# Nine weight buffers, six PSUM banks for the last expert job, per-tile turns, and a new order in a two-layer mixture-of-experts kernel

## The reference

```
x = x + L0_attn(L0_cond(x))        # attention with conditioning, then rotary attention (16 heads of 64)
x = x + L0_ffn(L0_cond2(x))        # quaternion filter, then 8 experts, top 2 of each token
x = x + L1_attn(L1_cond(x))        # 8 experts of three layers, top 2; then log-linear attention (8 heads of 128)
x = x + L1_ffn(L1_cond2(x))        # attention with conditioning, then a quantised FFN with a short convolution

# L0_ffn, a mixture: for each expert e
h = relu(x @ W1[e] + b1[e]);  y = h @ W2[e] + b2[e];  out += y * router_weight[:, e]
# L1_cond, a mixture: gate from rms-normalised x
h1 = relu(x @ W1[e]); h2 = relu(h1 @ W2[e]); out_e = h2 @ W3[e];  out = sum over the top 2
```

## Time and profile before

| | us |
|---|---|
| median of 3 runs (629.35, 630.21, 632.31) | 630.21 |
| the profiled execution, whole time | 623.68 |
| its span, first to last instruction | 621.9 |
| TensorE busy | 473.9 (76%) |
| VectorE busy | 303.5 (49%) |
| ScalarE busy | 246.2 (40%) |
| GpSimd busy | 171.4 (28%) |
| mean granted TensorE clock, share of full speed | 0.884 |

### The profile page before, as it was taken

One profiled execution on the slowest core, in us unless ns is written; L12 is line 12 of the kernel. 1 busy time (PEld: TensorE's weight loads), 2 busy tenths in 40 slices (PEclk: granted clock), 3 DMA queues, 4 the chain that ended last, 5 costly groups with the idle time before them and its releaser, 6 DMA issues.

```text
span 621.9 us, 11762 instructions
## 1 busy us (share of the span) xinstructions
PE 473.9 (76%) x4233; PEld 375.1 (60%) x4233; DVE 303.5 (49%) x771; ACT 246.2 (40%) x683; POOL 171.4 (28%) x210
## 2 busy tenths in 40 slices
PE   4897989768989946587776978669998734778875
PEld 4685877557869924466665866544665624566432
DVE  3779655643334427511122247774554003776653
ACT  3545644314575541123332463232554422343311
POOL 5054343172220233550004003455100022232200
PEclk9999989975999977769998998876999985897888
DMA  7977540010444530137786663101263710000000
GB/s 246 325 203 148 160 135 2 2 43 18 132 130 124 154 90 22 47 94 201 185 214 198 171 185 93 27 9 42 61 172 90 182 50 18 2 3 0 1 9 9
DMA packets 50631, 62.13 MB, mean 100 GB/s; under 512 B 6704, under 2 KB 39664, under 8 KB 50320
## 3 DMA queue, kind: packets, MB, share of 16 engines
q1 hardware_dynamic: 48048, 56.88, 33.1%
q0 software_dynamic: 2048, 4.20, 2.3%
q10 hardware_dynamic: 480, 0.32, 0.2%
HBM read 52.86 MB, written 16.94 MB: 112 GB/s over the span
## 4 chain that ended last, share of the span: by engine, by line
PE 55%; DVE 18%; issue 10%; ACT 10%; POOL 3%; another core or an unknown queue 2%; DMA 2%; ACTq 0%; POOLq 0%; DVEq 0%
PE PS L852 6%; PE PS L842 6%; PE PS L826 4%; PE PS L1407 4%; PE PS L1439 4%; PE PS L1834 3%; PE PS L1224 2%; PE PS L1238 2%; PE PS L1421 2%; DVE arena L1735 2%; PE PS L838 2%; PE PS L1213 2%; ACT rot_sm L1494 2%; ACT hid L920 2%
## 5 line engine op out<-in xcount | busy, mean ns | idle before, releaser
L766 POOL DMA_INDIRECT picked<-slots_y,place_u x32 | 31.1, 971 | 109.4 <-DMA slots_y<-slot_y 100.9
L852 PE MATMUL PS<-expert_w,hid 128*128 128x128 f32 x360 | 54.0, 287 | 7.6 <-ACT hid L920 2.7
L852 PEld LDWEIGHTS PS<-expert_w,hid 128*128 128x128 f32 x360 | 46.4, 196 | 14.4 <-issue 10.0
L1072 DVE TENSOR_SCALAR hid<-PS,expert_w 128x128 f32<-128x128 f32 x60 | 18.3, 347 | 75.3 <-PE PS L842 42.2
L842 PE MATMUL PS<-hid,expert_w 128*128 128x128 f32 x240 | 35.7, 296 | 12.5 <-ACT hid L920 9.9
L920 ACT ACTIVATE hid<-PS,expert_w 128x128 f32<-128x128 f32 x120 | 37.4, 366 | 16.7 <-PE PS L826 10.6
L842 PEld LDWEIGHTS PS<-hid,expert_w 128*128 128x128 f32 x240 | 31.3, 204 | 17.0 <-issue 15.8
L826 PE MATMUL PS<-slot_xT,expert_w 128*128 128x128 f32 x240 | 40.0, 293 | 1.9 <-ACT slot_xT L910 1.9
L1439 PE MATMUL PS<-rot_W,rot_yT 128*128 128x128 f32 x256 | 34.3, 298 | 3.7 <-ACT rot_yT L1509 3.7
L1439 PEld LDWEIGHTS PS<-rot_W,rot_yT 128*128 128x128 f32 x256 | 32.8, 211 | 6.9 <-ACT rot_yT L1509 5.7
L826 PEld LDWEIGHTS PS<-slot_xT,expert_w 128*128 128x128 f32 x240 | 33.6, 202 | 4.8 <-ACT slot_xT L910 2.7
(11 more groups left out here) (277 smaller groups left out, 1058.1 us busy)
## 6 DMA issues: line engine op xcount, KB each, us to landing
expert_w<-packed SPq DMA_DIRECT2D x60, 514.0 KB
slot_x<-slots_x SPq DMA_DIRECT2D x60, 64.0 KB
slots_y<-slot_y SPq DMA_DIRECT2D x60, 64.0 KB
packed<-in_moe_w_dram SPq DMA_DIRECT2D x6, 512.0 KB
packed<-in_moe_w_dram SPq DMA_DIRECT2D x3, 1024.0 KB
packed<-in_moe_w_dram SPq DMA_DIRECT2D x1, 2048.0 KB
slots_x<-zeros SPq DMA_DIRECT2D x2, 960.0 KB, 10.4
rot_qk<-in_attn_qk_dram SPq DMA_DIRECT2D x1, 1024.0 KB, 5.1
```

The lines of the kernel that those rows point to most:

```text
L766: nc.gpsimd.indirect_dma_start(picked[:, j, n, :], None, ys[half], bass.IndirectOffsetOnAxis(place_u[job % 2][:, j, n:n + 1], 0)).then_inc ...
L852: mm = nc.tensor.matmul(full(bank_of(MO_, i), 2 * P, 3 * P), hid[:, i % 2, c, :], W[i % WB][:, lo + E * (c - first):lo + E * (c - first) + ...
```

## The change

Five things are changed together.

First, the weights get nine buffers from job 1 on (`WMORE = 9`). The six new ones are cut from tiles that the rotary attention no longer needs: three from `rot_qk`, one each from `rot_yT`, `rot_W` and `rot_wqk`. Their first loads wait until the last rotary tile is done (`f_ready`). Slots of jobs 1 to 3 go round all nine; a load for slot i then waits for slot i - 9.

Second, job 3 uses other PSUM banks: 2 for turned rows, 1 and 3 for `hidden_a`, 7 and 4 for `hidden_b`, 5 for the output; and cond 1 of the last tiles uses banks 0 and 7 in place of 0 and 1.

Third, `transpose_x`, `copy_x`, `transpose_u` and `copy_u` are done tile by tile, each waiting for its own tile's `combine`, and `squares` moves from two VectorE instructions over four tiles to one ScalarE instruction with accumulation for each tile.

Fourth, several load semaphores are merged: the three attention weights share `attn`, the blanks, biases, cond 1 weights and packed weights share `late`, FFN weights, log weights and level masks share `log`.

Fifth, the whole table `TIMES` is new. All instructions stay the same otherwise; their order on each engine changes.

In the new order the gates and the log-linear work of half 0 stand behind job 2's slots instead of among them, and cond 1 and FFN work of tiles 2 and 3 stands behind job 3's slots, partly or whole.

The diff, cut. Of the table, one step's entries are shown as an example:

```diff
-    "m_transpose_x": (223.3, 367.5),
+    "m_transpose_x": (233.19, 234.04, 234.88, 235.89, 355.14, 357.05, 358.91, 360.45),
...
         WB, XB, YB = 3, 4, 3
 
-        MT_, MA_ = ((1, 1), (2, 3), (2, 2), (1, 1)), ((1, 1), (0, 1), (0, 1), (1, 1))
-        MB_, MO_ = ((7, 7), (7, 4), (7, 7), (7, 7)), ((7, 7), (6, 5), (6, 6), (7, 7))
+        WMORE = 9
+
+        MT_, MA_ = ((1, 1), (2, 3), (2, 2), (2, 2)), ((1, 1), (0, 1), (0, 1), (1, 3))
+        MB_, MO_ = ((7, 7), (7, 4), (7, 7), (7, 4)), ((7, 7), (6, 5), (6, 6), (5, 5))
 
         MM_ = (7, 7, 2, 7)
...
+        flat = [qk[:].rearrange("p s k c t -> p (s k c t)"), yT[:].rearrange("p h b t -> p (h b t)"), rW[:].rearrange("p h e -> p (h e)"), wr[:].rearrange("p k c t -> p (k c t)")]
+        W += [flat[m][:, (NW + FF0 // P) * c:(NW + FF0 // P) * (c + 1)] for m, c in ((0, 0), (0, 1), (0, 2), (1, 0), (2, 0), (3, 0))]
+        WBIAS = [w[:, NW:NW + FF0 // P] for w in W]
...
-            sp.dma_start(wv_in, d["attn0_v"]).then_inc(loaded["attn_vo"], 16)
-            sp.dma_start(wo_in, d["attn0_out"].rearrange("(c p) e -> p c e", p=P)).then_inc(loaded["attn_vo"], 16)
+            sp.dma_start(wv_in, d["attn0_v"]).then_inc(loaded["attn"], 16)
+            sp.dma_start(wo_in, d["attn0_out"].rearrange("(c p) e -> p c e", p=P)).then_inc(loaded["attn"], 16)
...
+        def buffer_of(i):
+
+            if i < SLOTS:
+                return i % WB, i // WB + 1, i - WB if i >= WB else None
+            b, turn = (i - SLOTS) % WMORE, (i - SLOTS) // WMORE
+            early = len(range(b, SLOTS, WB)) if b < WB else 0
+            last = range(b, SLOTS, WB)[-1] if b < WB else None
+            return b, early + turn + 1, i - WMORE if turn else last
+
+        def weights(i):
+            return W[buffer_of(i)[0]]
+
+        def weights_there(i):
+            b, uses, _ = buffer_of(i)
+            return w_loaded[b], 16 * uses
...
+                b, _, before = buffer_of(i)
                 if i == 0:
-                    sp.wait_ge(loaded["packed"], 16 * PACKS)
-                if i >= WB:
-                    sp.wait_ge(m_out_ps, i - WB + 1)
+                    sp.wait_ge(loaded["late"], LATE)
+                if before is not None:
+                    sp.wait_ge(m_out_ps, before + 1)
+                elif i >= WB:
+                    sp.wait_ge(f_ready, TILES)
                 if s < EXPERTS:
                     here = packed[layer][s:s + 1]
                 else:
                     sp.wait_ge(extra_ready, job + 1)
                     e = sp.value_load(extra[job % 2][0:1, s - EXPERTS:s - EXPERTS + 1], min_val=0, max_val=EXPERTS - 1)
                     here = packed[layer][bass.DynSlice(e, 1)]
-                sp.dma_start(W[i % WB][:], here.rearrange("o p f -> p (o f)")).then_inc(w_loaded[i % WB], 16)
+                sp.dma_start(W[b][:], here.rearrange("o p f -> p (o f)")).then_inc(w_loaded[b], 16)
...
-            def transpose_x(half):
-                pe.wait_ge(m_done, HT * (2 * half + 1))
-                if half:
-                    pe.wait_ge(routing, 4 * half)
-                claim(pe, (MX_[half],), (routing, 4 * half + 2))
-                for n in range(HT):
-                    mm = nc.tensor.transpose(full(MX_[half], P * n, P * n + P), xres[:, HT * half + n, :], k["ident"])
-                mm.then_inc(routing, 1)
+            def transpose_x(t):
+                half, n = divmod(t, HT)
+                pe.wait_ge(m_done, HT * 2 * half + n + 1)
+                if half and n == 0:
+                    pe.wait_ge(routing, 2 * half)
+                claim(pe, (MX_[half],), (mx_ready, t + 1))
+                nc.tensor.transpose(full(MX_[half], P * n, P * n + P), xres[:, t, :], k["ident"]).then_inc(mx_ps, 1)
...
+            def squares(t):
+                half, n = divmod(t, HT)
+                act.wait_ge(m_done, HT * 2 * half + n + 1)
+                nc.scalar.activation(sq[:, n, :], xres[:, t, :], ACT.Square, accum_out=st8[:, 0, n:n + 1]).then_inc(square_ready, 1)
+
+            def copy_u(t):
+                half, n = divmod(t, HT)
+                act.wait_ge(u_ps, t + 1)
+                nc.scalar.activation(uT[:, P * t:P * t + P], full(MU_[half], P * n, P * n + P), ACT.Copy).then_inc(u_ready, 1)
...
-            def squares(half):
-                dve.wait_ge(m_done, HT * (2 * half + 1))
-                here = xres[:, HT * half:HT * half + HT, :]
-                nc.vector.tensor_tensor(sq, here, here, ALU.mult).then_inc(mix_step, 1)
-                dve.wait_ge(mix_step, own_mix.next())
-                nc.vector.tensor_reduce(st8[:, 0, :], sq, X, ALU.add).then_inc(square_ready, 1)
...
-        COND_BANKS = ((0, 1) * 2 + (0,) * 4, (0,) * 4 + (0, 1) * 2)
+        COND_BANKS = ((0, 1) * 2 + (0,) * 4, (0,) * 4 + (0, 7) * 2)
...
-                pe.wait_ge(gating, 8 * (n // HT) + 2)
+                pe.wait_ge(u_ready, n + 1)
```

404 lines of the change are left out of this document (195 added, 209 removed), and 114 rows, old and new, of the table TIMES.

## The result

The changed kernel takes 588.13 us (583.58 to 595.95, 6 runs) against 630.62 us (623.79 to 633.51, 6 runs). The ratio is 0.9456, 95% interval 0.938 to 0.953. That is 5.4% faster; I had said 601 us, within 583 to 625. Every ratio in this document compares the fast executions of both kernels alone, while each median takes in all of them, so the two medians by themselves give another figure, 0.933.

The account below looks back on a forecast made before the run. It took TensorE (55% of the chain) as the bound, but unevenly, with idle parts to win. Terms +5 - 4.8 - 15 - 6.5 - 8 + 0 + 0 = -29.3 from 623.7 gave 594.4 profiled, 601 us median; range 583 to 625.

Parts of the forecast that it names:

- Step 1: End of job 0: rotary tails of tiles 6 and 7 now precede the last outputs; +5 us, range 0 to +12.
- Step 2: Hand-over from job 0 to job 1: fewer VectorE steps, faster combine, shorter POOL wait; -4.8 us, range -9 to 0.
- Step 3: Job 1: paired slots cover relu waits, period 3.35 to 2.5 us, weights loaded ahead; -15 us, ends 0 and -20.
- Rival C: Slots keep about 3 us, held by transfers or relus; jobs 1 to 3 gain little; median 616 us, chance 0.18.
- Step 4: Job 2: log-linear work leaves, the 5.16 us stall stays; -6.5 us, ends 0 and -17.
- Step 5: Job 2 to end of job 3: more banks, overlapping slots, a third of 24.8 idle us; -8 us, ends 0 and -20.
- Step 6: Gather of job 3 and tail: moved work fills the 15.0 us hole; 0 us, range -5 to +8.
- Step 7: Merged load semaphores: first readers wait for the last of a group; 0 us, range 0 to +1.3.
- Rival D: Slot rows, stores and gathers queue behind weight loads, period 4.2 us in jobs 1 and 2; median 642 us, chance 0.08.
- Rival B: With nine buffers filled ahead, slots of jobs 1 to 3 go at TensorE's pace; median 581 us, chance 0.13.
- Rival E: Whole kernel: what jobs 1 and 2 gain, job 0's end and the tail give back; 630 us, chance 0.03.

Follow-up runs that it names:

- old_order: The changed kernel with the order table of before (nine buffers, six banks in job 3, turns tile by tile, merged semaphores kept): 671.98 us, ratio 1.075.
- old_early: As old_order, with each weight load from job 1 on issued as early as nine buffers allow: 674.45 us, ratio 1.071.
- taps_late: The changed kernel with POOL's last spread of the FFN taps moved behind the gathers of job 0: 588.81 us, ratio 0.949.
- half_w: The changed kernel with weight loads of jobs 1 and 2 bringing half their bytes (wrong results, as many matmuls): 589.67 us, ratio 0.9443.
- banks_single: The changed kernel with one PSUM bank in place of two for each hidden half in job 3: 594.08 us, ratio 0.963.

## Why the prediction was right, and where it was not

The sum was near (-29.3 forecast, -31.5 in the profiled spans), and that is in part luck. By the stages of the table, +17.8 us of errors in one direction stand against -20.0 in the other, and the pair of profiles shows a smaller gain than the medians (42.5 us).

**Step 1, end of job 0, +5: wrong in place and size.** I let the rotary tails lengthen job 0. Job 0 took 77.1 us against 77.4, but not because its idle time took them in: the stage has 786 matmuls in both kernels. The new order put as much earlier work ahead of job 0, so that its first turn came 11.8 us late. Its end came 11.5 us late, just inside my range of 0 to +12. Windows of the first stage and of job 0, before and then after:

```profile
0.00:144.40 144.40, 115.47 (x1302) 96.28 (x1302) 91.43 (x201) 62.23 (x147) 56.85 (x68) 0.92 0.49 137
144.40:221.80 77.40, 70.62 (x786) 63.88 (x784) 31.20 (x60) 47.49 (x142) 16.98 (x17) 0.94 0.43 118
```

```profile
0.00:156.20 156.20, 124.43 (x1381) 104.23 (x1381) 104.04 (x218) 71.96 (x169) 59.59 (x72) 0.89 0.45 127
156.20:233.30 77.10, 71.53 (x786) 63.67 (x786) 28.59 (x55) 45.96 (x134) 11.92 (x13) 1.00 0.40 111
```

79 more matmuls and 9.0 us more of busy TensorE, part of it the lower clock, stand ahead of the first slot; the hand-over has 83 fewer (59 for 142). All seven profiles with the new first stage start job 0 at 152.0 to 157.3 us; with the old one it is 142.5 to 144.4, or 151.6 and 153.8 where the clock fell (old_order and old_early, with POOL's long wait, left out). I had read the order at the end of job 0 and not at its start.

**Step 2, the hand-over, -4.8: mis-sized, -1.0.** The two VectorE steps went and the combine of 1.96 us is 0.35 now, yet from the first gather to the first scatter are still 21.6 us, 1.1 less than before. POOL's wait for the places, which I had let shrink by 1.9, grew from 6.27 to 7.53. And the gather starts 2.7 us later, 2.0 of it by POOL's taps (taps_late). I had counted what SP is moved past, not what the gather is moved behind on POOL. Behind the last scatter the first turn came 2.7 us sooner, which I had not counted either.

**Step 3, job 1, -15: near in size, -12.8, by the wrong bound.** I took 2.5 us a slot because of 2.45 us of DMA time; it is 2.33 us, and half of the bytes give 2.33 as well. That the figure was near is luck: TensorE's busy time happened to be of the same size, 2.42 us in the earlier trace rows and 2.17 now. The pairs hide the relus, as said. What I had in passing, that nine buffers only take the start of a load off the slot, was too little: with four, the period is 2.67 us and job 2 is 23 us longer. Rival C is out: the period is not near 3, and the DMA share that it asked for did go to 0.98 without being the bound. That all transfers run on the same 16 engines, as the Trainium skill says, page "DMA: Bandwidth & Descriptors", section "Issuing engines are not separate DMA queues", no run here puts in doubt; that they were full here was my reading, and it was wrong.

**Step 4, job 2, -6.5: right**, -8.6 by the turns. The log-linear work is out of it (its first `project` starts at 367.52 us, behind the last output). The stall stayed, with the slow output behind it, as I had left it:

```profile
341.08 0.45 PE L847 MATMUL PS<-const,slot_x 128*128 128x128 f32 x1 [5.04 <-remote]
341.32 1.93 PE L881 MATMUL PS<-expert_w,hid 128*128 128x128 f32 x8
```

A second of 3.00 us came in job 1; without it job 1 would have been nearer to -16. The rows that the late turn reads were asked for at 324.64 us, 16 us ahead of it. VectorE stands at the same time, put down to "remote" as well, while POOL's gathers go on:

```profile
340.86 0.61 DVE L1099 TENSOR_SCALAR hid<-PS,rot_qk 128x128 f32<-128x128 f32 x2 [6.58 <-remote]
338.16 0.95 POOL L795 DMA_INDIRECT picked<-slots_y,place_u  x1 [0.30 <-issue]
```

Halving the bytes does not take this away. half_w has the same pause in job 2, only that TensorE's part of it is named "issue" and stands ahead of an output, which reads no rows; in job 1 it has 1.83 us:

```profile
337.36 2.05 PE L850 MATMUL PS<-expert_w,hid 128*128 128x128 f32 x8 [4.70 <-issue]
337.02 0.61 DVE L1068 TENSOR_SCALAR hid<-PS,expert_w 128x128 f32<-128x128 f32 x2 [6.63 <-remote]
```

In the last four profiles, on the other chip, neither engine waits for "remote" in jobs 1 and 2, with full loads.

**Step 5, from job 2 to the end of job 3, -8: too small, -19.5**, at its bound of -20. I had worked out that 13 us of TensorE work leave this stage and 6.5 come in, and then left the difference out of the sum and took a third of the idle time alone. Both were too little. From job 2's last output to job 3's, TensorE is busy 94.1 us where it was 103.3, so 9.2 us of work left on balance, and its idle time fell from 24.8 to 14.5. In job 3 by itself it is busy 51.45 us where it was 58.04, so 6.6 of the 15.8 us are work, and the other 9.2 are its 9.7 idle us, nearly all; the second bank for each half is 2 of these (banks_single). The part ahead of job 3 (56.7 us) is long in this profile: in the five others with the same order and nine buffers it took 52.1 to 53.9 us, so this term is more likely beyond its bound than at it.

**Step 6, the tail, 0: right**, -1.1. The hole took the work: 89.3 us of busy TensorE stand behind job 3 where it was 77.5.

**Step 7, the semaphores, 0: right in the new order, and not free.** ScalarE's first reader (L1490) starts at 16.13 us, waiting for the output weights to land, where its like started at 17.32 before. What I missed is that cond 1's weights wait with the packed ones; that costs nothing only because the order was made for it (27.06 us of wait otherwise).

Rival D is out: in jobs 1 and 2 no turn behind the first is put down to a load of rows, and no `hidden_a` to one of weights. Rival B came nearer than I allowed: what it named, slots at TensorE's pace, is what half_w leaves, its period of 2.1 us at a clock of 1.00 was 2.33, and the median of 588.13 us is closer to its 581 than to my 601. Rival E, that gains are given back elsewhere, had one true part, the 11.8 us at the start.

## What to carry to other kernels

An order, its buffers and its banks are one change: here the order with four buffers gave nothing (0.997), and buffers and banks without the order made it slower (1.024), while together they give 0.946. When instructions move, compare the work ahead of every milestone, the first one as well, and on every queue what the moved step now stands ahead of. Before calling an engine the bound, halve its load: a DMA share of 0.98 was no bound here. And count a pause by its time and its neighbours, not by the name of its releaser.
